# Graph attention on one core: two more V tiles per block on POOL, two tiles' logit sums on ACT, and a first part of Q loaded earlier

## The reference

```python
# x: (6250, 512); src (destination rows) and dst (columns) of 100,000 edges; 8 heads of 64
h = layernorm(x)
q, k, v = h @ Wq + bq, h @ Wk + bk, h @ Wv + bv
logits = einsum('ehd,ehd->eh', q[rows] / 8, k[cols]) + edge_attr
p = exp(logits - segment_max(logits, rows)[rows])
y = segment_sum(p / segment_sum(p, rows)[rows] * v[cols], rows)
x = x + y @ Wo + bo
x = x + ffn(layernorm(x))      # three small layers on decoded flags
```

## Time and profile before

| | us |
|---|---|
| median of 3 runs | 3242.53 (3241.57 to 3242.64) |
| the profiled execution | 3243.5 |
| its span, first to last instruction | 3241.7 |

### The profile page before, as it was taken

The page is one execution under the profiler, slowest core; times in us unless marked ns, Lnnn a source line. Parts: engine busy times, 40 slices in busy tenths (PEclk is TensorE's granted clock), DMA queues, the critical chain, the costliest instruction groups (busy, mean ns, idle before and its releaser), DMA issues.

```text
span 3241.7 us, 62767 instructions
## 1 busy us (share of the span) xinstructions
PE 2890.7 (89%) x11939; PEld 1687.3 (52%) x11939; DVE 2847.3 (88%) x20435; ACT 2108.6 (65%) x7365; POOL 2263.5 (70%) x2562
## 2 busy tenths in 40 slices
PE   4899888888888278999999999999999999989998
PEld 3555554454555134555555555555555555554444
DVE  8997777767777378999999999999999999998887
ACT  8332222222222037999999999999999999974444
POOL 0477777777777746888888888888888888861121
PEclk6798899988888688999999999999999999999999
DMA  6343443433333487888888888888888888841222
GB/s 189 78 138 108 106 112 108 114 103 99 109 108 97 132 312 247 270 263 268 261 270 266 265 265 265 269 265 261 271 265 266 264 265 269 262 142 61 84 79 71
DMA packets 259601, 619.75 MB, mean 191 GB/s; under 512 B 62433, under 2 KB 80493, under 8 KB 258958
## 3 DMA queue, kind: packets, MB, share of 16 engines
q0 software_dynamic: 144832, 443.72, 43.6%
q1 hardware_dynamic: 110862, 164.95, 17.0%
q10 hardware_dynamic: 3520, 7.08, 0.6%
HBM read 553.68 MB, written 61.92 MB: 190 GB/s over the span
## 4 chain that ended last, share of the span: by engine, by line
DVE 46%; POOL 23%; issue 14%; PE 12%; DMA 2%; DVEq 1%; ACT 1%; SPq 0%; POOLq 0%
DVE big L1361 26%; POOL rec_scratch L673 23%; DVE big L1470 12%; PE banks L2024 5%; PE banks L2089 2%; DVEq L1470 1%; DVE big L1081 1%; DVE big L1455 1%; PE banks L2003 1%; PE banks L2012 1%; PE banks L1947 1%; DMA big<-kv_scratch,small 1%; DVE ext L1439 1%; PE banks L2092 1%; DMA big<-in_edge_attr_dram 1%
## 5 line engine op out<-in xcount | busy, mean ns | idle before, releaser
L886 ACT ACTIVATE big<-big,small 128x65 f32<-128x65 f32 x6164 | 1508.8, 340 | 5.1 <-DMA big<-kv_scratch,small 0.4
L1361 DVE SCALAR_TENSOR_TENSOR big<-banks,big 128x64 f32<-128x64 f32 x6656 | 1030.6, 214 | 35.8 <-PE banks L1947 18.0
L694 POOL DMA_INDIRECT big<-kv_scratch,small x832 | 844.5, 1015 | 280.7 <-DVE big L1361 133.0
L673 POOL DMA_INDIRECT rec_scratch<-big,small x782 | 773.7, 989 | 324.5 <-issue 237.9
L1947 PE MATMUL banks<-big,small 128*128 x1664 | 892.7, 619 | 44.2 <-DVE big L1361 35.0
L2003 PE MATMUL banks<-big,small 128*128 128x260 f32 x3328 | 882.9, 388 | 44.3 <-DVE big L1470 22.1
L2003 PEld LDWEIGHTS banks<-big,small 128*128 128x128 f32 x3328 | 616.3, 190 | 449.7 <-issue 289.9
L1470 DVE SCALAR_TENSOR_TENSOR big<-big,loS,banks 128x520 f32 x832 | 619.6, 745 | 6.3 <-PE banks L2003 4.1
L1838 PE MATMUL banks<-big 128*128 128x512 f32 (+1 forms) x1176 | 598.0, 656 | 22.2 <-DVE big L1071 22.2
L702 POOL TENSOR_SCALAR small<-iotaF,small 128x128 f32<-128x128 f32 x832 | 527.9, 635 | 65.8 <-PE banks L2003 39.0
L1361 DVE DVE_READ_ACCUMULATOR big<-banks,big 128x1 f32 x6656 | 522.7, 79 | 0.1
(11 more groups left out here) (274 smaller groups left out, 2733.7 us busy)
## 6 DMA issues: line engine op xcount, KB each, us to landing
rowR<-lo_rows SPq DMA_DIRECT2D x97, 256.0 KB
big<-src_rows SPq DMA_DIRECT2D x97, 256.0 KB
big<-in_x_dram SPq DMA_DIRECT2D x96, 256.0 KB, 4.1
big<-kv_scratch,small POOLq DMA_INDIRECT x832, 5.3
rec_scratch<-big,small POOLq DMA_INDIRECT x782
kv_scratch<-big SPq DMA_DIRECT2D x48, 260.0 KB
q_scratch<-big SPq DMA_DIRECT2D x48, 256.0 KB
kv_scratch<-big SPq DMA_DIRECT2D x48, 256.0 KB
```

Source lines behind the costliest of these rows:

```text
L673: e.indirect_dma_start(recd, bass.IndirectOffsetOnAxis(ap=ridx[:, c % 4, j:j + 1], axis=0), rec[:, 8 * c + j, :], None).then_inc(s_sc[c % ...
L694: e.indirect_dma_start(KV[:, vat(t):vat(t) + YW + D], None, KVd, bass.IndirectOffsetOnAxis(ap=recB[b_ % 4][:, t % 16, 9:10].bitcast(i32), ...
L886: ins = e.activation(heads(Vr(t), h, h + 1), heads(Vr(t), h, h + 1), ACT.Copy, scale=ph[:, h:h + 1])
L1361: ins = e.scalar_tensor_tensor(k_, QB[t % 2][:, 64 * h:64 * h + 64], 1.0, k_, ALU.mult, ALU.mult, accum_out=Lr[t // 16 % 2][:, t % 16, h:h ...
```

## The change

- `on_pool` holds for t % 16 in (6, 10, 14) and no longer for 10 alone: 151 tiles in place of 50. POOL does `pvp(t)` in step t + 25, just ahead of the tile's `one_hot(t)`, and no longer in step t + 21.
- For t % 16 in (3, 9), up to tile 792 (99 tiles), `kq` is one 128x512 product on DVE without accumulator output, and ACT takes the eight sums: `sums(t)`, eight 128x64 copies in place with an accumulator output, in ACT's step t + 3. `gather` and `lb` also wait for them (`s_sum`).
- The first piece of Q is 11 windows in place of 8 and is loaded as soon as the projections are stored and the last row of the sort's inputs is in; the three other pieces of ACT's queue go out where all four did. The projections' units end four chunks earlier, with a third unit in 12 chunks and no longer in 4.

```diff
-        for c in range(2, NCH):
-            for k in range(3 if c in (12, 24, 36, 48) else 2):
+        for c in range(2, NCH - 4):
+            for k in range(3 if c % 7 == 6 and c < 90 else 2):
...
-        QW = ((0, 8), (8, 16), (16, 24), (24, 27), (27, 33), (33, 40), (40, 49))
+        QW = ((0, 11), (11, 16), (16, 24), (24, 27), (27, 33), (33, 40), (40, 49))
...
-        on_pool = [t % 16 in (10,) and t < LAST for t in range(T)]
+        summed = [t % 16 in (3, 9) and t < LAST - 16 for t in range(T)]
+        sum_at = [sum(summed[:t + 1]) for t in range(T)]
+        s_sum, sum_base = s_ab, 2 * NCH
+        on_pool = [t % 16 in (6, 10, 14) and t < LAST for t in range(T)]
...
                 q.wait_ge(s_rd, k + 1)
+                if k >= 0:
+                    q.wait_ge(s_sum, sum_base + sum_at[k])
...
                 if s - DEL - 2 >= 0:
+                    if on_pool[s - DEL - 2]:
+                        pvp(s - DEL - 2)
                     one_hot(s - DEL - 2)
-                if 0 <= s - DEL + 2 < T and on_pool[s - DEL + 2]:
-                    pvp(s - DEL + 2)
...
+            def load_q(k):
+
+                w0, w1 = QW[k]
+                e.dma_start(Qall[:, w0:w1, :], Qd[128 * w0:128 * w1, :].rearrange("(w p) n -> p w n", p=128)).then_inc(s_q[k], 16)
+
             q.wait_ge(s_pj, 3 * W)
+            for i in range(3):
+                q.wait_ge(s_st[i], 16 * W + 16)
+            q.wait_ge(s_rl[0], q_base[0])
+            load_q(0)
             q.wait_ge(s_psel, NCH)
...
-            for k in range(4):
-                w0, w1 = QW[k]
-                e.dma_start(Qall[:, w0:w1, :], Qd[128 * w0:128 * w1, :].rearrange("(w p) n -> p w n", p=128)).then_inc(s_q[k], 16)
+            for k in range(1, 4):
+                load_q(k)
...
+            def sums(t):
+
+                q.wait_ge(s_rd, t + 1)
+                q.wait_ge(s_x2, t // 16 - 1)
+                for h in range(8):
+                    k_ = Kr(t)[:, 64 * h:64 * h + 64]
+                    ins = e.activation(k_, k_, ACT.Copy, accum_out=Lr[t // 16 % 2][:, t % 16, h:h + 1])
+                ins.then_inc(s_sum, 1)
...
                 b_, r_ = s // 16 - 1, s % 16
+                if 3 <= s < T + 3 and summed[s - 3]:
+                    sums(s - 3)
                 if s >= DEL and not on_pool[s - DEL]:
                     pva(s - DEL)
...
+                if summed[t]:
+                    if not half:
+                        e.tensor_tensor(Kr(t), QB[t % 2], Kr(t), ALU.mult).then_inc(s_rd, 1)
+                    return
...
                 q.wait_ge(s_rd, 16 * b_ + 16)
+                q.wait_ge(s_sum, sum_base + sum_at[16 * b_ + 15])
```

## The result

| | before | after |
|---|---|---|
| median of 4 runs, us | 3242.05 (3241.17 to 3242.64) | 3445.98 (3440.63 to 3447.93) |
| profiled execution (span), us | 3243.5 (3241.7) | 3444.51 (3442.7) |
| gathers start, first to last, us | 1130.5 to 2860.4 | 1128.0 to 3058.6 |

The changed kernel is slower: ratio 1.0628, 95% interval 1.0615 to 1.0642, some 204 us. The forecast was 3341 (3235 to 3410): the right direction and half the size.

A forecast was written before the change was run, and what follows sets the result against it. DVE was taken to set the pace at 32.75 us a block, with POOL and ACT near it. Median 3242.5, +96 for a 35.0 us ring (mean excess 2.0 over 47 blocks) and +3 for start-up gave about 3341 us (3235 to 3410).

The forecast's parts named there:

- the ring: Attention: gather(14) waits for tile 9's sums in ACT's queue, closing a loop of 35.0 us a block against 32.75; chance 0.71.
- R(6): The moment DVE ends kq of step 6; ACT's next instruction was put 3.14 us later, gather(14) 11.0 us later.
- both bounds (1.3 and 3.4): Lowest and highest cost in us of one tile's eight sums on ACT; 1.9 was taken.
- A wrapped lane: In 5 of 35 tiles gather(15) is held in place of gather(14), 1.85 us less: 33.2 us a block.
- To the gather's start, as in the 0.28 above: 0.2.: POOL: from the end of ACT's sums of tile 9 to the start of gather(14), 0.2 us.
- From the start of kq(4): DVE: from the start of kq(4), when gather(4)'s data land, to the next R(6), 5.9 us.
- Landing: 5.0.: K/V DMA: gather(4)'s data take 5.0 us to arrive, between the shortest, 4.3, and the median, 5.3.
- V multiply placed just before its own one-hot ... Nothing added.: POOL: the later V multiply costs nothing beyond its 2.86 us steps, as PE wants it only about 3 us after the gather.
- POOL pacing: Rival: POOL alone sets the attention's pace at 32.7 us a block, 3240 us in all; chance 0.11.
- DVE pacing: Rival: DVE keeps the attention's pace and each block gains its 1.07 us, 3190 us in all; chance 0.12.
- Tile 3 is harmless: ACT's sums of tile 3 end at 2029.7, POOL reaches gather(8) at about 2029.6, so they hold nothing up.
- The sum is unhidden on ACT: Rival: sums cost ACT 3.4 us a tile, its own queue starts the loop, 38 us a block, about 3475 us; chance 0.06.

The follow-up runs named there:

- b2_v_ahead: The changed kernel with POOL's V multiply four steps ahead of its one-hot again (t + 21), sums as in the change: 3428.54 us beside 3243.76, ratio 1.0574.
- d1_sums_t2_quiet_v: The changed kernel with sums in ACT's step t + 2 and V tiles 10, 12, 14 in POOL's steps 11, 13, 15: 3364.16 us beside 3243.76, ratio 1.0377.
- a2_sum9: The changed kernel with only tile 9 of each block summed on ACT: 3707.54 us beside 3488.65, ratio 1.0613.
- a1_no_sums: The changed kernel with no tile summed on ACT, still three V tiles a block on POOL: 3575.45 us beside 3488.65, ratio 1.0259.
- b4_no_sums_quiet_v: The changed kernel without sums on ACT, V tiles 10, 12, 14 in POOL's steps 11, 13, 15: 3497.68 us beside 3478.99, ratio 1.0056.
- b1_sums_early: The changed kernel with the sums in ACT's step t + 1 in place of t + 3: 3524.26 us beside 3478.99, ratio 1.0136.
- a3_sum3: The changed kernel with only tile 3 of each block summed on ACT: 3565.51 us beside 3488.65, ratio 1.0197.

## Why the prediction was half right

**What was right.** The mechanism and its place, by the working and not by luck. gather(14) waits for the sums of tile 9 behind ACT's queue; tile 9 alone gives the whole loss. Of the ring's terms, R(6) to ACT's next instruction was put at 3.14 us and measures 3.15 (R(6) at 2020.21, pva from 2023.36); three pva tiles 5.75 and 5.75; a sum 1.9 and 1.91, so the pva pitch was the right row, and both bounds (1.3 and 3.4) can go, as can the 1.2 us a tile without the read: ACTIVATE and read come every 0.24 us together (the 334 ns beside it should read 333, which changes nothing); POOL from gather(14) to gather(0), one plain and one V step, 4.71 and 4.70. A wrapped lane saves 1.9 us in one block of seven, for the 1.85 that was forecast. Units and Q cost nothing, the 128x512 product takes 0.665 us for the 0.62 to 0.69 taken, the start-up moved nothing that stands out.

**What failed, term by term.** The forecast ring was 35.0, the measured one 37.17. In the forecast's own four stretches:

- R(6) at 2020.21 to gather(14) at 2031.86: 11.65 for 11.0.
- gather(14) to gather(4) at 2007.81: 13.12 for 13.1.
- gather(4) to the start of kq(4) at 2013.70, called landing: 5.89 for 5.0.
- The start of kq(4) to R(6): 6.51 for 5.9.

The third is not a landing. The data of gather(4) were in after 5.2 us, and DVE, which has no idle time between kq(0) and kq(4), came later. So the path has to be followed over kq(0), and on it four terms make the difference:

| stretch | forecast | changed kernel | b2_v_ahead |
|---|---|---|---|
| gather(14) to gather(0) | 4.71 | 4.70 | 4.70 |
| gather(0) to the start of kq(0) | 5.0 | 5.52 | 5.13 |
| kq(0) to the copy of step 4 | 8.69 (before), less 0.53 | 8.86 | 9.30 |
| copy of step 4 to copy of step 8 | 8.85 (before) | 9.09 | 8.91 |
| that copy, three pva tiles, sums(9) | 8.13 | 8.16 | 8.13 |
| end of the sums to gather(14) | 0.2 | 0.84 | 0.85 |
| ring | 35.05 | 37.17 | 37.02 |

The forecast column is written out now, over kq(0), with the lengths of before and with the 0.53 of tile 3 taken off, as if it lay on the path; the text went over kq(4) and came to 35.0. Each column is one block; b2_v_ahead's starts at 2026.14, and there kq(0) waits last for PE and not for its data. The lengths of before come from these rows, kq(0) and `carries` on DVE and the copies of steps 4 and 8 on ACT:

```profile
2018.32 0.21 DVE L1361 SCALAR_TENSOR_TENSOR big<-banks,big 128x64 f32<-128x64 f32 x1
...
2024.88 0.16 DVE L1405 TENSOR_TENSOR_SCAN ext<-small,ext 8x17 f32<-8x17 bf16 x1
```

```profile
2027.01 0.60 ACT L839 ACTIVATE small<-banks 128x512 f32<-128x512 f32 x1 [1.24 <-PE banks L1957]
...
2035.86 0.57 ACT L839 ACTIVATE small<-banks 128x512 f32<-128x512 f32 x1
```

1. *"To the gather's start, as in the 0.28 above: 0.2."* The row it came from was a release by DVE. A release by ACT takes 0.84 here from the last sum's slot, and 0.74 to 0.77 from its end in every ring read (0.71 of "issue" in the chain of d1_sums_t2_quiet_v). +0.64.
2. *"From the start of kq(4)".* The step that failed is to let kq(4) start when the data of gather(4) land; DVE's own queue brings it there later. On that queue the ring leaves DVE at `carries` (line 1434, 2011.65, step 3) and goes over a small product of PE to the rows and ACT's copy at 2013.77, 2.12 us; before the change it was 2.13 (2024.88 to 2027.01). kq(3) at 2011.74 comes behind `carries`, so its 0.53 is off the path, and up to `carries` DVE took 0.18 longer (`back1` 0.60 for 0.42 us). +0.7.
3. *"Landing: 5.0."* kq(0) starts 5.52 after gather(0); the median landing of all gathers went from 5.3 to 5.4. The argument that a gather behind a V step lands earlier did not hold. +0.5.
4. *"V multiply placed just before its own one-hot ... Nothing added."* The text named PE's demand as the only thing that could be touched, and left out that POOL's multiply and DVE's small operations use one port. `last_max` took 1.34 us in this block and 0.47 in that of before, and that is what lengthens the stretch from kq(4) to R(6) from 5.9 to 6.51. On the ring it is worth 0.2 to 0.3 (9.09 against 8.91 and 8.85), since ACT's own queue, with tile 3's sums in it, covers the rest. In a2_sum9 those sums are gone and the hold-up takes their place (9.94). Each covers for the other; the ring with neither, tile 9 alone and V in quiet steps, was not run. Without the ring it is the largest term: 1.6 us a block between a1_no_sums and b4_no_sums_quiet_v. The forecast's sums for POOL pacing (32.7 a block) and for DVE pacing (31.7) lacked it: a1_no_sums has no ring and took 34.6, and with the sums' 1.07 off DVE that makes an estimated 33.6, which is what b1_sums_early took.

These make 2.1 of the 2.12 us. The mean over all blocks is 36.9 and not 37.2 because of the wrapped lanes.

*"Tile 3 is harmless"* held for the changed kernel's V steps (a3_sum3) in so far as it makes no ring. But gather(8) does wait for its sums (1.26 us at 2017.35), and its 1.9 us are in the 8.91 of ACT's queue between the copies. It does not hold in general: d1_sums_t2_quiet_v is a ring over tile 3.

**The range.** Its upper end, 3410, came from a longer sum and a landing of 5.3. No bound was put on the release or on the port, and the landing was tied to one median. A bound of 0.84 could not be had from a row of before, but a whole unknown release deserved one; that DVE's small lines read SBUF twice could be seen in the operands of their groups (small<-rowR,ext,small for `last_max`).

**Rivals.** POOL pacing and DVE keeping pace are out: POOL waits for ACT and DVE falls to 91%. "The sum is unhidden on ACT" is out by its price, but its path was half right: from the copy of step 4 to that of step 8 ACT's own queue is busy for all but 0.16 us in the changed kernel, and for all of it in b2_v_ahead.

**Where the lateness is decided.** With the change's amounts a block takes 33.6 us with sums at t + 1 (33.8 with V quiet), 35.2 at t + 2 (V quiet), 36.9 at t + 3. At t + 2 the change's own V steps were not run, nor were quiet ones at t + 3. Earlier than t + 1 there is nothing to sum. ACT then waits 2 to 2.4 us a block for DVE, so at these amounts no placement tried beats the kernel before.

## What to carry to other kernels

Where several engines are within 5% of full (here DVE, PE and ACT) and tied by short rings, work moved off the fullest one is paid in the latency of the new hand-over: close the ring before counting busy time, and follow it over the engine that really carries each stretch (here PE and ACT, so that a saving on DVE fell beside it). Before moving a two-input operation to POOL, list the DVE operations with both inputs in SBUF that run in the same steps, and place it among the others; then look again at which gathers it now delays.

## What the runs showed of the hardware

- A DVE operation with both inputs in SBUF that meets POOL's tensor_tensor (1.07 us) waits it out, small as it may be: 8x1 elements took a mean of 1,125 ns instead of 206. The trace shows it as a longer operation, not as idle time, so busy shares hide it: DVE looked full at 199.6 of 200 us in a1_no_sums. It loses even when its recorded start is ahead: 2051.17 against 2051.57 for POOL, and it took 1.64 us for POOL's 1.08.
- An indirect DMA on POOL starts 0.74 to 0.77 us after the end of the ACT instruction that releases it, against 0.27 to 0.28 after DVE and 0.17 us behind POOL's own last instruction when it waits for nothing.
- On ACT a 128x64 copy with an accumulator output is two instructions, 241 and 188 ns, that overlap to 0.24 us a pair.
